# Spacing the row scatters of the first expert layer over the attention steps that run beside them

## The reference, cut to what matters

```python
x = x + attention(layernorm(x))     # x: [2048, 256], 16 query heads, 4 key heads, width 16, causal,
                                    # scores -> 50 * tanh(scores / 50) -> softmax
x = x + ffn(layernorm(x))           # 64 experts, 6 per token, 96 slots per expert, plus a shared expert
x = x + gated_scan(layernorm(x))
x = x + ffn(layernorm(x))

# inside ffn, the part that matters here (K = 6, C = 96 slots, T = 2048 tokens):
topk_w, topk_i = top_k(masked_scores, K)
pos  = position of this choice among all choices of the same expert
slot = expert * C + min(pos, C - 1)
buf  = zeros((E * C, H)).at[slot].set(x[tok])      # each token's row goes to six slots
out  = experts(buf)                                # then each expert works on its 96 slots
```

## Time and profile before

| | |
|---|---|
| median of three timed executions | 1483.82 us |
| profiled execution, its own time | 1465.4 us |
| profiled execution, span from first to last instruction | 1463.6 us |
| mean granted TensorE clock over the span | 0.857 of 2.4 GHz |
| PE busy | 1058.7 us (72%) |
| PEld busy | 627.3 us (43%) |
| ACT busy | 709.3 us (48%) |
| DVE busy | 519.1 us (35%) |
| POOL busy | 386.9 us (26%) |

### The profile page before, as it was taken

One profiled execution on the slowest core, in us unless ns is written; L12 is line 12 of the kernel. 1 busy time (PEld: TensorE's weight loads), 2 busy tenths in 40 slices (PEclk: granted clock), 3 DMA queues, 4 the chain that ended last, 5 costly groups with the idle time before them and its releaser, 6 DMA issues.

```text
span 1463.6 us, 18870 instructions
## 1 busy us (share of the span) xinstructions
PE 1058.7 (72%) x6648; PEld 627.3 (43%) x6648; DVE 519.1 (35%) x1557; ACT 709.3 (48%) x921; POOL 386.9 (26%) x336
## 2 busy tenths in 40 slices
PE   5868777876877587575559988467777534799874
PEld 3533233322322132123359977344444312698762
DVE  7752421551213122103323322146454432133226
ACT  2368989895999599493024433023020200244330
POOL 3000000024000600600535644103241516365450
PEclk9889889898999889787879999689786757799995
DMA  9970000002000200004847998811310232489977
GB/s 355 393 277 0 1 1 1 15 32 78 1 1 15 88 15 1 19 0 113 243 86 175 288 254 209 243 60 55 141 70 30 83 96 63 92 200 285 257 184 290
DMA packets 94925, 176.11 MB, mean 120 GB/s; under 512 B 13118, under 2 KB 46879, under 8 KB 94832
## 3 DMA queue, kind: packets, MB, share of 16 engines
q1 hardware_dynamic: 71216, 146.48, 31.9%
q0 software_dynamic: 23616, 28.44, 9.4%
HBM read 107.30 MB, written 83.72 MB: 131 GB/s over the span
## 4 chain that ended last, share of the span: by engine, by line
PE 22%; DMA 8%; issue 8%; DVE 5%; another core or an unknown queue 4%; SPq 3%; DVEq 1%; ACT 1%; POOL 0%; POOLq 0%; ACTq 0%
PE PS L1303 9%; DMA WD_space<-in_wd 6%; PE PS L1314 5%; PE PS L1375 2%; SPq L1082 2%; PE PS L1241 1%; PE PS L1290 1%; PE PS L1341 1%; SPq L1083 1%; DMA spare_space<-expert_out 1%; PE PS L1228 1%; DMA XE<-expert_in 1%; DMA expert_out<-ob,yidx 0%; POOL expert_out L1193 0%
## 5 line engine op out<-in xcount | busy, mean ns | idle before, releaser
L293 POOL DMA_INDIRECT expert_in<-xp,didx x192 | 187.2, 975 | 771.5 <-DVE didx L280 586.0
L659 ACT ACTIVATE PR<-PS 128x1024 f32<-128x1024 f32 (+3 forms) x320 | 275.0, 930 | 109.4 <-remote 38.3
L664 ACT ACTIVATE PR<-PR 128x2048 f32<-128x2048 f32 (+3 forms) x160 | 271.5, 1699 | 0.0
L567 PE MATMUL PS<-PR,V 128*32 128x512 f32 (+3 forms) x1280 | 171.5, 597 | 88.4 <-ACT PR L664 84.4
L1193 POOL DMA_INDIRECT expert_out<-ob,yidx x128 | 180.7, 1411 | 182.0 <-ACT ob L1475 137.5
L555 PE MATMUL PS<-QT,KT 96*128 96x512 bf16 (+3 forms) x640 | 181.6, 378 | 52.9 <-ACT PR L659 42.1
L1303 PE MATMUL PS<-XT,WGU 128*88 128x96 f32 x1600 | 152.6, 249 | 18.9 <-DMA WD_space<-in_wd 18.1
L1303 PEld LDWEIGHTS PS<-XT,WGU 128*88 128x88 f32 x1600 | 147.6, 159 | 36.9 <-DMA WD_space<-in_wd 25.6
L555 PEld LDWEIGHTS PS<-QT,KT 96*128 96x128 bf16 x640 | 59.1, 104 | 166.3 <-ACT PR L659 114.9
L1657 DVE SCALAR_TENSOR_TENSOR gta<-gth,PS 88x192 f32<-88x192 f32 x128 | 44.8, 350 | 222.5 <-ACT gth L1465 183.9
L1465 ACT ACTIVATE gth<-PS 88x192 f32<-88x192 f32 x128 | 41.9, 328 | 132.6 <-PE PS L1303 131.4
(11 more groups left out here) (245 smaller groups left out, 1350.8 us busy)
## 6 DMA issues: line engine op xcount, KB each, us to landing
WGU<-in_wgu SPq DMA_DIRECT2D x100, 352.0 KB
WD_space<-in_wd SPq DMA_DIRECT2D x100, 176.0 KB
expert_out<-zero SPq DMA_DIRECT2D x2, 8256.0 KB, 50.4
expert_in<-zero SPq DMA_DIRECT2D x2, 7776.0 KB, 39.3
XE<-expert_in SPq DMA_DIRECT2D x32, 486.0 KB
spare_space<-expert_out SPq DMA_DIRECT2D x24, 512.0 KB, 5.3
spare_space<-in_wgu SPq DMA_DIRECT2D x20, 352.0 KB
normed<-xp SPq DMA_DIRECT2D x8, 512.0 KB, 2.9
```

The source lines that it names most:

```text
L293: pool.indirect_dma_start(out=buf_d[f], out_offset=bass.IndirectOffsetOnAxis(ap=didx[b][:, r, j:j + 1], axis=0), in_=xp[b][:, r, :], in_of ...
L567: last = pe.matmul(PS[VW * j:VW * (j + 1), AV0 + unit % 2, cols(c, s):CW], V[:, g, s, :], PR[:, n % 3, j, cols(c, s):CW], start=(s == 0), ...
L659: act.activation(PR[:, n % 3, 2 * pr:2 * pr + 2, cols(c, s):CW], PS[:, S0 + 2 * pr:S0 + 2 * pr + 2, cols(c, s):CW], ACT.Tanh, scale=1.0 / ...
L664: act.activation(PR[:, n % 3, :, lo:CW], PR[:, n % 3, :, lo:CW], ACT.Exp, scale=SOFT_CAP).then_inc(exp_done, 1)
```

## The change

`dispatch_rows` gets a third argument `paced = (first, per)`. With it, each of the 24 scatters first waits on GpSimd for `exp_done` to have reached `first + i // per`, where `i` is the number of the scatter. `exp_done` reaches `n + 1` when the exp of head step `n` is done.

The three calls in the first block become: chunk 0 one scatter per step from `first_step(2, 0) + 28` = 76, chunk 1 one per step from `first_step(3, 0) + 22` = 118, chunk 2 two per step from `first_step(3, 0) + 47` = 143. The calls in the second block stay as they are.

```diff
-        def dispatch_rows(pool, k):
+        def dispatch_rows(pool, k, paced=None):
             f, b = k // NC, k % NXP
             pool.wait_ge(rows_ready, k + 1)
             pool.wait_ge(routed, k + 1)
             for r in range(CT):
                 for j in range(TOPK):
+                    if paced:
+                        pool.wait_ge(exp_done, paced[0] + (r * TOPK + j) // paced[1])
                     pool.indirect_dma_start(
                         out=buf_d[f], out_offset=bass.IndirectOffsetOnAxis(ap=didx[b][:, r, j:j + 1], axis=0),
                         in_=xp[b][:, r, :], in_offset=None, bounds_check=E * CAP - 1, oob_is_err=False)\
...
                 pool.wait_ge(cleared, 64)
-                for k in range(K0):
-                    dispatch_rows(pool, k)
+                dispatch_rows(pool, 0, (first_step(2, 0) + 28, 1))
+                dispatch_rows(pool, 1, (first_step(3, 0) + 22, 1))
+                dispatch_rows(pool, 2, (first_step(3, 0) + 47, 2))
```

## The result

The changed kernel took 1421.16 us (median of 4 executions, 1413.56 to 1428.03), the kernel before 1479.09 us beside it. The ratio is 0.960, 95% interval 0.9525 to 0.9676: faster, and inside the forecast range of 1410 to 1456. The profiled execution took 1413.56 us against 1465.4, 51.8 less.

The account below looks back on a forecast made before the run. ScalarE bounds attention, with TensorE held during three scatter bursts. Removing 50.3 us of holes, with all other terms at 0, takes 1483.82 us to 1433.5, 3.4% faster; range 1410 to 1456 us.

Parts of the forecast that it names:

- The bound: First block's attention: ScalarE sets the pace; during scatter bursts TensorE stops progressing after some ten scatters and scores come late.
- The removed holes, 50.3 us: ScalarE's idle holes beside the three first-block bursts, 14.75, 17.56 and 18.00 us, vanish: 50.3 us gained.
- The upper bound of 55.8: Cross-check in attention: key heads with bursts against quiet heads, differences 16.7, 19.9 and 19.2, at most 55.8 us gained.
- Spaced scatters hold nothing: First block, chunks 0 to 2: scatters at one or two per step leave 0 us of the holes.
- The likening to the sends at 60% of GpSimd's time: Experts' stretch, 757 to 845: 39 sends kept GpSimd 60% busy without holding TensorE; both new scatter rates lie below.
- The estimate of a backlog that empties at over 80 rows per us: Bursts: what fills over ten scatters empties about 4 us after 24, so faster than the paired chunk's 71 rows per us.
- the 0 for the paired chunk: Chunk 2, two scatters per step: no hole left, 0 us, with 18.0 us as the other bound.
- The end of the scatters: End of first block: chunk 2's last two scatters end some 12 us before attention's last exp; cost 0.
- The rule: Skill's sentence that DMA and compute cannot slow each other: scatters don't hold TensorE, holes stay, 1483.8 us.
- The paired third chunk: Rival, chunk 2: two scatters per step still stall, 18.0 us of holes stay, 1451.5 us; chance 0.13.
- no spaced scatter held anything up: Answers the slower rival: each spaced scatter holds TensorE in 60 steps, 104 us lost for 50 gained, 1537 us; chance 0.03.
- The rival that the holes are not the scatters' doing: First block's bursts: something else stops TensorE, or spacing doesn't matter; 1484 us or a few less; chance 0.06.

Follow-up runs that it names:

- second comparison: The changed kernel, unaltered, run again beside the kernel before on a chip where bursts delay TensorE's results: 1424.79 us against 1476.13, ratio 0.966.
- g1: Changed kernel with chunk 0 unbroken, 24 plain DMAs added, chunk 1 in clusters of 12, chunk 2 of 8: 1453.55 us, ratio 0.987 to the kernel before.
- e1: Changed kernel, but each chunk's 24 scatters wait only for their first step, then go back to back: 1358.86 us, ratio 1.001 to the kernel before.
- e2: Changed kernel, but two scatters per step in chunks 0 and 1 as well: 1361.24 us, ratio 0.999 to the kernel before.
- e3: Changed kernel at the same mean rate, but scatters in clusters of 8 back to back: 1362.58 us, ratio 1.000 to the kernel before.
- e4: Changed kernel at the same mean rate, but scatters in clusters of 12 back to back: 1358.43 us, ratio 0.999 to the kernel before.
- f1: Repeat of the changed kernel with late start and 24 scatters back to back, on another chip: 1362.79 us, ratio 1.000 to the kernel before.
- f2: Repeat of the changed kernel with clusters of 12 scatters back to back, on another chip: 1364.79 us, ratio 1.003 to the kernel before.

## Why the prediction was right, step by step

- *The bound.* Right that attention's pace was set by ScalarE's work and, in the bursts, by scores that reached ScalarE late. Misread was the cause one step back: TensorE did not stand still by itself before 341.67 and 613.11, it waited for ScalarE, and what was late was the update for scores issued long before. What makes it late is not known.
- *The removed holes, 50.3 us.* Measured 51.8 between the two profiled executions, 52.2 in the tanh group, 51.3 between the medians of the second comparison. In the first comparison the medians differ by 57.9; with four executions that spread over 14 us, the interval on the ratio is 48 to 70 us of gain. The upper bound of 55.8 was not reached in the profiles. It set the two heads with bursts against the shorter of chunk 3's two quiet heads, 55.3 us; the other, from 537.27 to 594.58, took 57.3, and against that one the three differences are 16.7 + 17.8 + 17.2 = 51.7, close to what was measured. Since the forecast took 1483.82 for the kernel before and the comparison found 1479.09, part of the 12 us between forecast and result is the base.
- *Spaced scatters hold nothing.* Right for one and for two per step; no hole over 1.6 us in ScalarE's timeline from 290 us to the end of attention. The likening to the sends at 60% of GpSimd's time gave the right answer. The estimate of a backlog that empties at over 80 rows per us is not borne out as a law of rows: 24 plain DMAs pass 128 rows every 0.54 us and hold nothing. What g1 bears out is its weaker form, that some ten scatters without a break are free and a pause of 5 us resets. So the 0 for the paired chunk was the right answer from a model that no run bears out; that part was luck.
- *The end of the scatters.* The last pair's wait was foreseen to end at 654.2 on the old clock, 603.9 with 50.3 taken off; the pair started at 601.34, 2.6 us earlier, and ended at 602.62 + 0.97 = 603.6. Attention's last exp ended at 613.61 + 1.73 = 615.3, so the scatters ended 11.7 us before it, as foreseen (12). No wait took the place of the holes.
- *The rule.* "A DMA cannot be slowed by a compute op, and vice versa" (the Trainium skill, SBUF — State Buffer, "SBUF: two separate sides") was given 0.06. What the rival made of it holds on the second kind of chip and for the plain burst on the first; for scatters on the first kind it fails, 20.7 us in one burst of g1. The section speaks of the ports to SBUF, and no run shows that the delay arises at a port, so the sentence itself may stand.
- *The rivals.* The paired third chunk has no holes; no spaced scatter held anything up. The rival that the holes are not the scatters' doing fell on the first kind. But it had a form that the prediction did not think of: on the second kind the kernel has no holes to remove. The changed kernel itself was not run there; its variants e1 to e4, f1 and f2 range from 1358 to 1365 us against 1360, so I expect no change there. The forecast was right for the kind of chip that the profile came from, and that the comparison ran on that kind was luck.

## What to carry to other kernels

Before costing background work at nothing because its engine is idle, look for late semaphore updates ("remote") on the engines beside it. Break up long rows of indirect DMAs from GpSimd (eight, then some 5 us of pause, or one or two per step of other work), but keep the whole row shorter than the time until the next one. When an engine seems to stand still, look whether the kernel makes it wait for the engine that is late. And compare the kernel before on more than one chip before a gain is taken as the kernel's: here it was 3.4 to 4% on one kind, and on the other nothing that could be measured in its variants.

## What the runs showed of the hardware

On three of the five chips of the experiments, an unbroken row of indirect scatters from GpSimd (128 rows of 1296 bytes every 1.28 us) lets TensorE's results come late from about the tenth on, until some 4 us after the last. It isn't the volume: the third burst of the kernel before moved 0.67 MB, the first 3.98 MB, and it had holes of 18.0 us against 14.75. ScalarE's and GpSimd's own instructions kept their durations. On two chips the same rows hold nothing up. The number of rows that is written does not matter, then; whether the number of rows named or of scatters counts was not run.

One more thing differs between the two kinds, counted in the traces themselves. Each scatter makes 16 updates of its semaphore, 384 in a burst. The trace of the kernel before has 95 of the 384 of its first burst, the one of e1 has 368. On the first kind nearly all of the changed kernel's spaced scatters of chunk 0 have their 16 each, while in that first burst most have one to six; the 24 plain DMAs of g1 have all 384. So on the first kind of chip the records of semaphore updates go missing in the same bursts in which updates come late. The data itself isn't late: the last packet of the first burst starts 2.1 us after the last scatter in both. Whether updates back up in the chip, or whether recording them is part of the trouble, stays open, as does what differs between the chips: every execution timed here left a record, so there is none without one to compare with. It also means that "remote" there can stand for an update whose record is missing; what shows the holes is the time at which ScalarE's instructions start.
